# Two graph layers in fp32 on one core: another spread of the layer-2 tiles, and four banks for the chains of the last chunk

## What is computed

```python
h = maximum(layernorm(x), 0) @ W0 + B0
mask = (adj < 0.5) & ~eye
r = where(mask, adj, 1.0)
S = where(mask, exp(-(1/r - 1/mu)**2 / (2 sigma**2)), 0)
x = x + S @ h                                   # layer 1
h = maximum(layernorm(x), 0) @ W1.T
x = x + (adj * adj + eye) @ h                   # layer 2
```

## Time and profile before

| | |
|---|---|
| median of 3 runs | 1880.04 us (1878.95 to 1880.99) |
| the profiled execution | 1879.75 us, span of the trace 1877.9 us |
| TensorE busy | 1840.0 us, 98% of the span |
| VectorE busy | 1723.2 us, 92% |
| ScalarE busy | 1730.2 us, 92% |
| HBM traffic | 497 MB, mean 265 GB/s |
| granted TensorE clock | 0.995 of full speed |

### The profile page before, as it was taken

One profiled execution on the slowest core, in us unless ns is written; L12 is line 12 of the kernel. 1 busy time (PEld: TensorE's weight loads), 2 busy tenths in 40 slices (PEclk: granted clock), 3 DMA queues, 4 the chain that ended last, 5 costly groups with the idle time before them and its releaser, 6 DMA issues.

```text
span 1877.9 us, 13284 instructions
## 1 busy us (share of the span) xinstructions
PE 1840.0 (98%) x4820; PEld 879.6 (47%) x4820; DVE 1723.2 (92%) x1012; ACT 1730.2 (92%) x986; POOL 87.6 (5%) x110
## 2 busy tenths in 40 slices
PE   7999999999999999999999999999999999999998
PEld 4544444444444444444444444444444444555565
DVE  7999999999999999999999999999999955678686
ACT  8999999999999999999999999999999997777562
POOL 0000000000000000000000000000000000000011
PEclk9999999999999999999999999999999999999999
DMA  8476878987878787777677776666666578667997
GB/s 312 163 292 260 326 281 305 323 294 285 307 269 324 235 297 258 251 275 257 245 253 266 258 286 239 242 219 229 220 227 218 191 265 287 248 251 259 309 353 226
DMA packets 83138, 497.85 MB, mean 265 GB/s; under 512 B 9601, under 2 KB 10241, under 8 KB 26881
## 3 DMA queue, kind: packets, MB, share of 16 engines
q1 hardware_dynamic: 68832, 469.33, 65.4%
q0 software_dynamic: 14096, 27.53, 8.4%
q10 hardware_dynamic: 144, 0.13, 0.0%
HBM read 469.17 MB, written 27.79 MB: 265 GB/s over the span
## 4 chain that ended last, share of the span: by engine, by line
PE 43%; ACT 32%; DVE 18%; issue 6%; DMA 1%; SPq 0%; DVEq 0%; ACTq 0%
PE p_x L468 12%; PE p_l1b L434 11%; ACT rings L778 10%; ACT rings L783 9%; ACT rings L788 9%; PE p_l1a L434 8%; PE p_own L468 7%; DVE rings L611 6%; DVE rings L604 6%; DVE rings L622 3%; ACT rings L796 2%; PE p_x L446 1%; PE p_x L448 1%; PE p_x L447 1%; DVE high L639 1%
## 5 line engine op out<-in xcount | busy, mean ns | idle before, releaser
L611 DVE SCALAR_TENSOR_TENSOR rings<-rings,small 128x2048 f32<-128x2048 f32 x256 | 600.5, 2346 | 29.0 <-ACT rings L783 28.8
L604 DVE SCALAR_TENSOR_TENSOR rings<-rings 128x2048 f32<-128x2048 f32 x256 | 585.1, 2286 | 8.2 <-PE p_l1b L434 6.8
L788 ACT ACTIVATE rings<-rings,small 128x2048 f32<-128x2048 f32 x256 | 533.0, 2082 | 34.3 <-DVE rings L611 33.9
L778 ACT ACTIVATE rings<-rings,small 128x2048 f32<-128x2048 f32 x256 | 509.4, 1990 | 9.3 <-DVE rings L604 6.8
L468 PE MATMUL p_x<-rings,h 128*128 128x512 f32 x1128 | 505.4, 592 | 0.0
L783 ACT ACTIVATE rings<-rings 128x2048 f32<-128x2048 f32 x256 | 488.0, 1906 | 5.5
L434 PE MATMUL p_l1b<-rings,h 128*128 128x512 f32 x1024 | 460.9, 596 | 3.6 <-ACT rings L788 3.5
L434 PE MATMUL p_l1a<-rings,h 128*128 128x512 f32 x1024 | 459.5, 595 | 0.2
L468 PEld LDWEIGHTS p_x<-rings,h 128*128 128x128 f32 x1128 | 213.5, 190 | 261.1 <-issue 260.0
L622 DVE TENSOR_TENSOR rings<-rings 128x2048 f32<-128x2048 f32 x135 | 308.5, 2285 | 7.3 <-DMA rings<-adjT 4.6
L434 PEld LDWEIGHTS p_l1b<-rings,h 128*128 128x128 f32 x1024 | 194.3, 191 | 245.4 <-issue 236.9
(11 more groups left out here) (92 smaller groups left out, 498.9 us busy)
## 6 DMA issues: line engine op xcount, KB each, us to landing
rings<-adjT SPq DMA_DIRECT2D x439, 1024.0 KB, 6.9
outT<-xa_buf POOLq DMA_DIRECT2D x89, 256.0 KB, 5.7
x_buf<-xT SPq DMA_DIRECT2D x24, 256.0 KB, 6.7
outT<-y_buf POOLq DMA_DIRECT2D x15, 256.0 KB, 5.9
xa_buf<-xT SPq DMA_DIRECT2D x8, 256.0 KB, 5.9
outT<-x_buf POOLq DMA_DIRECT2D x1, 256.0 KB, 4.8
y_buf<-outT SPq DMA_DIRECT2D x1, 256.0 KB, 13.1
outT<-y_buf SPq DMA_DIRECT2D x1, 128.0 KB, 1.7
```

Of the source, the lines that this page charges most:

```text
L604: dve.scalar_tensor_tensor(out=tile(s_ring, slot_of(t)), in0=tile(a_ring, slot), scalar=CUTOFF, in1=tile(a_ring, slot), op0=ALU.is_lt, op1 ...
L611: dve.scalar_tensor_tensor(out=v, in0=v, scalar=neg_2c, in1=v, op0=ALU.add, op1=ALU.mult).then_inc(squared, 1)
L778: act.activation(v, v, ACT.Ln, bias=tiny_c).then_inc(ln_done, 1)
L788: act.activation(v, v, ACT.Exp, bias=exp_bias, scale=neg_k).then_inc(sens_done, 1)
```

## The change

Thirteen layer-2 tiles stand in most chunks instead of twelve, so 79 are left from the last chunk on instead of 90; three tiles of rows 12 and 13 (`KEPT`) are kept for the final chains of these rows, which now come first. The three tail items of their own kind (`TAIL`) are gone. Chains that begin at step 6 of the last chunk or later (`wide`) rotate over four banks and are copied up to six items after their end, but at least two items before their bank is used again. Of the tiles that may be split, those with `m % 7` not 1 or 4 are, 41 in all, instead of `m % 5` 0, 2 or 4. Diagonal tiles of the last chunk and the tail (`late`, six of them) are squared by ScalarE; VectorE adds the diagonal one item later. The premask of a step of the last chunk comes at its first item, and the row steps after the last layer-1 tile one step later. There are 98 chains and 446 tile loads. The diff, its core:

```diff
-QUOTA = [0, 10] + [12] * 13
+QUOTA = [0, 11, 13] + [12] * 3 + [13] * 9
-TAIL = 3
+END_ROWS = [12, 13, 0, 1, 2, 3, 4, 5, 6, 7, 8, 9, 10, 11, 14, 15]
+KEPT = [(12, 12), (12, 13), (13, 13)]
+WIDE_STEP = 6
+EVAC_WIDE = 6
+AHEAD = 2
@@ slots_of
-    n = NC * NC - 2 * NC + 1 - sum(QUOTA) - TAIL
-    return [(2 * k + 1) * NC // (2 * n) for k in range(n)] + [NC + k for k in range(TAIL)]
+    n = NC * NC - 2 * NC + 1 - sum(QUOTA) - len(KEPT)
+    return [(2 * k + 1) * NC // (2 * n) for k in range(n)]
@@ make_plan
-    done, chains, items, order = set(), [], [], [list(range(NC))]
+    done, chains, items, order = set(KEPT), [], [], [list(range(NC))]
...
-    ends = [Chain(row, [J for J in range(NC) if (row, J) not in done], True) for row in range(NC)]
+    done -= set(KEPT)
+    ends = [Chain(row, [J for J in range(NC) if (row, J) not in done], True) for row in END_ROWS]
     chains += ends
-    tail = [(ch, ch.sources[0]) for ch in ends[:OPEN]] + [(ch, ch.sources[1]) for ch in ends[:OPEN]]
+    tail = [(ch, J) for ch in ends[:OPEN] for J in ch.sources[:-1]] + [(ch, ch.sources[-1]) for ch in ends[:OPEN]]
     tail += [(ch, J) for ch in ends[OPEN:] for J in ch.sources]
-    items += [Item(ch.row, J, ch, S_STEPS + TAIL + k) for k, (ch, J) in enumerate(tail)]
+    items += [Item(ch.row, J, ch, S_STEPS + k) for k, (ch, J) in enumerate(tail)]
     for k, ch in enumerate(chains):
         ch.index = k
-        ch.bank = (k - len(chains) + NC) % OPEN if ch.final else k % 2
+        begin = min(it.step for it in items if it.chain is ch)
+        ch.wide = begin >= LAST + WIDE_STEP
+        ch.bank = (k - len(chains) + NC) % OPEN if ch.wide else k % 2
@@ SPLITS
-          and it.m % 5 % 2 == 0]
+          and it.m % 7 not in (1, 4)]
...
+    it.late = it.row == it.source and it.step >= S_STEPS - NC
+LATE = [it.m for it in ITEMS if it.late]
...
-        ch.evac = max(ch.last_m + EVAC, CHAINS[ch.index - 1].evac)
+        ch.evac = max(ch.last_m + (EVAC_WIDE if ch.wide else EVAC), CHAINS[ch.index - 1].evac)
+        if ch.wide:
+            ch.evac = min([ch.evac] + [o.first_m - AHEAD for o in CHAINS[ch.index + 1:] if o.bank == ch.bank])
@@ l2 (TensorE)
-                elif it.first and it.chain.final and it.chain.bank == 2 and it.chain.row < OPEN:
-                    pe.wait_ge(y_ready, NC - 2)
-                elif it.first and it.chain.final and it.chain.bank == 3 and it.chain.row < OPEN:
-                    pe.wait_ge(x1_added, NC - 1)
                 elif it.first and it.chain.after:
                     pe.wait_ge(xa_added, it.chain.after[-1].index + 1)
+                elif it.first and it.chain.bank == 2:
+                    pe.wait_ge(y_ready, NC - 2)
+                elif it.first and it.chain.bank == 3:
+                    pe.wait_ge(x1_added, NC - 1)
@@ VectorE
+            def add_late_eye(it):
+                dve.wait_ge(late_squared, LATE.index(it.m) + 1)
+                add_eye(a_ring, it.load % A_RING).then_inc(q_by["dve"], 1)
...
-                fast = c < NC - 1
-                if i == 3:
+                fast, end = c < NC - 1, c == NC
+                if i == (4 if end else 3):
                     add_x1(c - 1)
-                if i == (4 if fast else 5):
+                if i == (4 if fast else 6 if end else 5):
                     relu_row(c - 1)
...
-                if i == (6 if fast else 7 if c == NC else 8):
+                if i == (6 if fast else 8 if end else 8):
                     keep_h2(c - 1)
...
-                    if dense and it is AT_STEP[s][len(AT_STEP[s]) // 2]:
+                    if dense and it is AT_STEP[s][0]:
                         premask(s)
-                    if it.by == "dve":
+                    if it.by == "dve" and not it.late:
                         square_adj(it)
+                    if it.m and ITEMS[it.m - 1].late:
+                        add_late_eye(ITEMS[it.m - 1])
                     if it.m and ITEMS[it.m - 1].split is not None:
                         halves(ITEMS[it.m - 1])
...
@@ ScalarE
-                act.activation(a, a, ACT.Square).then_inc(q_by["act"], 1)
+                squares = act.activation(a, a, ACT.Square)
+                if it.late:
+                    squares.then_inc(late_squared, 1)
+                else:
+                    squares.then_inc(q_by["act"], 1)
...
-                    if it.by == "act":
+                    if it.by == "act" or it.late:
                         square_adj(it)
```

More of the change, by code:

```diff
@@ L301, in gnn_program @@
         q_by = {"dve": sem("q_by_dve"), "act": sem("q_by_act")}
+        late_squared = sem("late_squared")
         q_used = sem("q_used")
@@ L722, in row_steps @@
                     return
-                fast = c < NC - 1
-                if i == 3:
+                fast, end = c < NC - 1, c == NC
+                if i == (4 if end else 3):
                     add_x1(c - 1)
-                if i == (4 if fast else 5):
+                if i == (4 if fast else 6 if end else 5):
                     relu_row(c - 1)
-                if i == 5 and c >= 2:
+                if i == (5 if end else 5) and c >= 2:
                     add_y(c - 1)
-                if i == (6 if fast else 7 if c == NC else 8):
+                if i == (6 if fast else 8 if end else 8):
                     keep_h2(c - 1)
@@ L758, in _ @@
                     if it.m == len(ITEMS) - 1:
+                        if it.late:
+                            add_late_eye(it)
                         if it.split is not None:
```

## The result

The changed kernel takes 1871.2 us (median of 6 runs, 1869.4 to 1872.0), the kernel before 1879.9 in the same session. The ratio is 0.9951 with a 95% interval of 0.9939 to 0.9964: 9 us, half a per cent, faster. The forecast was 1872.7, range 1865 to 1880. The profiled execution has a span of 1869.6 us, 8.3 less. Times in this text are medians of executions at the usual pace; one of the four of e8 took 1930.8 us at a granted clock of 0.949 and is left out.

The account below looks back on a forecast made before the run. VectorE was taken to bound chunks 1 to 5 and TensorE the rest. 2.5 + 25.8 - 37.1 + (5 - 3.94) + (2.5 - 2.08) = -7.3 us on 1879.75, with 0.3 for the median, gave 1872.7, range 1865 to 1880.

Parts of the forecast that it names:

- Chunks 1 to 5: Early stretch: two added tiles lengthen it by 2.5 us, bounds nothing and 6.9.
- VectorE sets the pace: Chunks 1 to 5: VectorE, busy 501.3 of 506.1 us, was read as the bound, so its 2.4 us more work counted.
- the rival that I gave 0.12: A thirteenth tile costs its full price everywhere: 6.9 us early, 27.5 in chunks 6 to 13; 1878.8 us, chance 0.12.
- Chunks 6 to 13: Middle stretch, paced by TensorE: eight added tiles cost 25.8 us, bounds 25.3 to 27.5.
- Last chunk and tail: TensorE idle there rises from 3.94 to 5 us before row 15's normalisation and from 2.08 to 2.5 after it.
- the tail from T0: From the normalisation of row 15 to the last matmul: 85.5 us of matmuls plus 2.5 idle, 88.0 for 90.7.
- VectorE's copy waits: Last chunk: waits of 5.2 + 4.1 us for a chain's last matmul were expected to go through later copies from four banks.
- the diagonal squares: Last chunk and tail: six squares of 2.3 us each leave VectorE; a visible TensorE stall of 1.62 us near the end.
- The loads as the bound of the tail: Rival: loads at full rate keep the tail at 90.7 us instead of 88.0; 1875.4 us, chance 0.10.
- VectorE as the bound of the last chunk: Rival: VectorE's waits stay while its cover shrinks; 1889.3 us in full, chance 0.06, or 1881.0 by half, 0.07.
- All idle gone: Rival: nothing added early, 25.3 us in chunks 6 to 13, 2 us of idle left of 6.0; 1864.2 us, chance 0.10.
- the last two tiles: Sign for right, end of the tail: TensorE's last two tiles no longer stand apart, where it had waited 1.62 us.

Follow-up runs that it names:

- e8: The changed kernel with five more layer-2 squares on ScalarE instead of VectorE in chunks 1, 2, 3 and 5; 1869.2 us, ratio 0.9944.
- e9: The changed kernel without the two tiles added in chunks 1 and 2, still 41 splits; 1870.2 us, ratio 0.9949.
- e3: The changed kernel with wide chains copied 3 items after their end instead of 6; 1871.7 us, ratio 0.9956.
- e5: The changed kernel with the six diagonal tiles of the last chunk and tail squared by VectorE again, in line; 1876.0 us, ratio 0.9980.
- e6: The changed kernel with the premask of a last-chunk step back at the step's middle item; 1867.7 us, ratio 0.9937.
- e13: The kernel of e6 with the quotas of e9; 1868.1 us, ratio 0.9939.
- e10: The changed kernel with the final chains' accumulating stores cut to an eighth of their columns; 1869.4 us, ratio 0.9944.
- e12: The kernel of e6 with 6 of 7 eligible tiles split before the tail instead of 5 of 7, 45 splits; 1873.6 us.
- e2: The changed kernel with the old quotas, 90 tiles left from the last chunk on, 45 of them split; 1871.3 us, ratio 0.9952.
- e1: The kernel before with the new quotas alone, 79 tiles left and 38 splits; 1872.7 us, ratio 0.9960.
- e4: The changed kernel with the old rule for splits, 37 splits instead of 41; 1874.4 us, ratio 0.9968.

## Why the prediction was right, and which of its terms were not

The time is 1.5 us below the forecast, but three of its terms are off, by +4.1, -2.6 and -2.6 us, and partly cancel, so that it came this close is in part luck. Measured between TensorE's marks, the change is 2.8 us less work and 0.3 + 4.3 + 1.1 us less over work, 8.4 together (the rows of the table are rounded).

**Chunks 1 to 5: 2.5 expected for two tiles; wrong.** The step that failed is "VectorE sets the pace". It read a busy share of 99% as the bound. Seen from TensorE a tile costs its full 3.43 us there: the rival that I gave 0.12, true for this stretch and false for the middle. What stands over work there, some 13 us, is made by 5 to 7.5 us at the start of chunk 1, where no layer-2 tile exists (a wait of 3.1 to 3.6 us for row 0, and half the clock for some 3 to 5 us behind it), and by the rest in waits of 0.4 to 2.3 us at the rows' ends. e8 took 11 us off VectorE and e9 two tiles off the stretch without changing it. Two tiles bring 6.9 us of work, and the time over work is 0.3 less: 6.6 instead of 2.5, and the term was 4.1 too small. VectorE's row ends, by which I had cut, show only +4.5 us, since VectorE's lead over TensorE is not the same at both.

**Chunks 6 to 13: 25.8 expected, bounds 25.3 to 27.5; 23.2 measured.** The mechanism was right, the size of the idle was not. I took TensorE's idle from the busy column, 2.2 us, and so bounded the gain by it. Counting instructions gives 794.5 - 789.4 = 5.1. The column hides short pauses, because a tile that takes 3.43 us of the stream is drawn as 3.60. Of the 5.1, 4.3 went, so the gain of 27.5 - 4.3 = 23.2 lies below the lower bound.

**Last chunk and tail: idle up by 1.5 expected; down by 1.1 measured** (by 2.5 without the low clock of this execution). Work fell by 37.1 as counted, and the tail from T0 was forecast at 88.0 and is 87.9. But the forecast let VectorE's copy waits do the saving, and e3 shows that they were worth 1.0 us (one profiled execution, 0.5 by the medians). The part whose removal costs most is the one that I had called visible and priced at 1.6 us, the diagonal squares: e5 gives 3.9 in the profile and 4.8 in the time. The premask, which I had counted as a help to ScalarE, costs 1 to 2.3 there (e6, e8, e9, e13). I had named VectorE's waits for ScalarE and chain ends, and not the one that took their place: 6.8 us of waits for a slot of S in the last chunk before the change, 31.0 after it (from 1542.6 to 1765.3 and from 1570 to 1761). That VectorE would wait there could have been seen, since the S ring has three slots in the last chunk and TensorE's pace frees them.

**The rivals.** The loads as the bound of the tail: refuted by e10, where the rate fell from 354 to 333 GB/s and the DMA share from 1.01 to 0.93 and the tail stayed at 87.88 us. The loads need 81.5 us, by the working of the forecast, and the matmuls 85.5. The Trainium skill, "DMA: Bandwidth & Descriptors", Specifications, puts the limit of one core at about 358 GB/s. As a mean over the tail the trace agrees, 354; over 2 us it does not (430 from 1844 to 1846). VectorE as the bound of the last chunk: not at 41 splits, but the edge is near. At 45 in the shorter last chunk (e12) it costs TensorE more than the splits save; e2 carries 45 in the longer one. All idle gone: the middle all but did it (0.9 over work), the rest did not.

**The signs.** Of those named for "right", the row ends 102 us apart came, and so did the lack of idle there, TensorE's idle of 4 to 10 us and the last two tiles. VectorE's waits for chain copies are none from 1655 to T0 and 3.7 us behind it, where under 3 was named. The fifth row end came 5.0 us later instead of 2 to 3; the sign for "wrong", an early stretch longer by 5 or more, is missed at 4.5 by VectorE's row ends and met at 10.0 by TensorE's marks.

**The sum of halves.** The prediction treated the change as a list of gains. e1 and e2 show that they do not add: 7.4 us for the one, 8.8 for the other, 8.7 for both. Moving tiles forward takes them out of the only stretch in which this kernel makes a tile cheaper. That it also takes away what covers VectorE there is argued, not shown (e2).

What stays open: how the gain of the diagonal squares divides between the shorter list of VectorE and the lead at the very end; what four banks and the row order are worth by themselves, which no run separates; and how the 12 to 14 us over work in chunks 1 to 5 divide, beyond row 0.

## What to carry to other kernels

Find an engine's idle by counting its instructions against a mark in its own stream, not from its busy share; and test what sets the pace by taking work off the suspect, since 99% busy was no bound here. Price a part by what it puts in front of other work in an in-order list: of this change, a reordering that looked free cost about 2 us, and moving six squares off the list brought 4.8. Before adding up two gains, ask whether one uses up what the other works on.

## What was not expected of the hardware

A pause of TensorE of 2.58 us was followed, about 1 us after it had resumed, by 3 us of matmuls 0.43 us apart instead of 0.23 (e6, above). At the start of chunk 1 stands a wait of 3.60 us, and then two layer-1 tiles in 9.57 us instead of 6.87; there the clock is low from the moment that TensorE resumes (0.67 over 138 to 140). TensorE's timeline of the changed kernel, then its busy time by stretch there, with the granted clock third from the end:

```profile
138.84 1.87 PE L524 MATMUL p_stat<-mean_of,square_buf 128*128 128x1 f32 x8 [3.60 <-ACT square_buf L843]
...
140.57 9.57 PE L449 MATMUL p_l1b<-rings,h 128*128 128x512 f32 x16
```

```profile
140.00:145.00 5.00, 5.00 (x10) 2.42 (x10) 4.97 (x4) 4.97 (x6) 0.00 (x0) 0.50 0.59 213
```

A clock of 0.50 is the lower of its two levels, 1.2 of 2.4 GHz. So these two stalls cost 1.5 and 1.8 times what the wait itself shows: 2.58 + 1.4 us in the last chunk, 3.6 + 2.7 in chunk 1. But a pause of that length does not always bring it. e8 has the same stall in the last chunk, to the hundredth:

```profile
1720.79 0.47 PE L461 MATMUL p_own<-high,h_high 128*128 128x512 f32 x1 [2.58 <-DVE low L660]
```

```profile
1720.00:1725.00 5.00, 4.21 (x16) 3.01 (x17) 4.96 (x5) 4.80 (x3) 0.00 (x0) 1.00 0.20 26
```

The granted clock stays at 1.00 there, and e8's last chunk and tail are 1.4 us shorter for it, with the same code in them. In e12 the clock falls after the pause of 2.22 us (0.76 from 1718 to 1725) and not after that of 2.73, and in e1 it falls after one of 2.28 (0.50 from 1696.9 to 1699.9). So of these pauses of 2.2 to 2.8 us some were followed by the low clock and some were not, and a difference of 1.4 us between two executions that have them says nothing about the kernels. In the last chunk and tail the clock fell before the last matmul in the profiled executions of the changed kernel, e1, e3, e4, e5, e10 and e12, and in no other.
